# A vision block's head on one core: the state-space addition in two halves, and maxima over partitions by DMA rows and VectorE

## The reference

```python
# 1. tokens: a diagonal state-space kernel, for each token h and example c a row of 1024
K = 2.0 * einsum('chn,hnl->chl', Cc, exp(dtA[:, :, None] * ell)).real        # h = (64, 128, 1024)
# 2. attention over the 128 tokens of each example, 32 heads of 32, 8 key/value heads, rope
h = h + attention(layernorm(h), wq, wk, wv, wo)
# 3. a dense layer with LoRA experts and a router
y = x @ W_base.T + b_base
contribs = (x @ lora_A[active].T) @ lora_B[active].T * 2.0
alpha = softmax(log(prior[active] + EPS) + (x @ router_W.T + router_b)[active])
h = h + y + sum(alpha * contribs)                                            # x here is layernorm(h)
```

## Time and profile before

| | |
|---|---|
| median of 3 executions | 3023.05 us (3019.66 to 3023.64) |
| the profiled execution | 3020.96 us, span 3019.1 us |
| mean granted TensorE clock | 0.973 |
| busy: TensorE, VectorE, ScalarE, GpSimd | 2840.1, 2468.1, 1897.5, 1968.4 us |

### The profile page before, as it was taken

How to read it: one execution, slowest core, us unless ns; L and a number is a source line. 1 busy time by engine, 2 the same in 40 slices (tenths; PEclk the granted TensorE clock), 3 DMA queues, 4 the chain that set the end, 5 groups by cost and what they waited for, 6 DMA issues and landing times.

```text
span 3019.1 us, 61979 instructions
## 1 busy us (share of the span) xinstructions
PE 2840.1 (94%) x16986; PEld 1410.7 (47%) x16986; DVE 2468.1 (82%) x8692; ACT 1897.5 (63%) x5933; POOL 1968.4 (65%) x1723
## 2 busy tenths in 40 slices
PE   3777699999999999999999999999999999999986
PEld 3555444444444444444444444444444444444432
DVE  7897578888888888888888888888888888888872
ACT  5775566666666666666666666666666666666651
POOL 3431377677677676677776677777777777767762
PEclk8988699999999999999999999999999999999998
DMA  7965466766666667666667666666666766666651
GB/s 199 214 173 164 88 139 145 145 146 153 147 142 151 150 143 153 147 146 148 146 145 152 148 147 148 146 150 147 151 149 140 152 146 146 152 147 145 143 121 53
DMA packets 1252719, 442.59 MB, mean 147 GB/s; under 512 B 1200144, under 2 KB 1208592, under 8 KB 1252512
## 3 DMA queue, kind: packets, MB, share of 16 engines
q1 hardware_dynamic: 1252512, 440.69, 66.2%
HBM read 88.22 MB, written 67.11 MB: 51 GB/s over the span
## 4 chain that ended last, share of the span: by engine, by line
PE 43%; DVE 21%; issue 13%; POOL 12%; ACT 8%; SPq 1%; DMA 1%; DVEq 1%; ACTq 0%; POOLq 0%
PE bank_b L1570 19%; PE bank_a L1570 13%; DVE heads L1363 5%; ACT probs L1166 5%; DVE probs L1309 5%; POOL p_hl L1085 4%; POOL probs L1081 4%; PE bank_c L1570 3%; PE kps L498 2%; PE score L1537 2%; POOL rope_a L1091 2%; DVE share L1318 2%; PE pv L1559 1%; POOL xy_hl L1100 1%; POOL z L262 1%
## 5 line engine op out<-in xcount | busy, mean ns | idle before, releaser
L1166 ACT ACTIVATE probs<-probs,negmax 128x128 f32<-128x128 f32 x2048 | 789.8, 387 | 262.5 <-DVE negmax L1309 262.4
L1085 POOL TENSOR_TENSOR p_hl<-probs,p_hl 128x512 f16<-128x512 f32 x512 | 615.7, 1203 | 344.6 <-ACT p_hl L1175 342.3
L1081 POOL TENSOR_TENSOR probs<-probs,rsum 128x512 f32<-128x512 f32 x512 | 556.7, 1087 | 221.4 <-DVE rsum L1320 220.3
L1570 PE MATMUL bank_a<-qkv_hi,xt 128*128 128x512 f16 x2048 | 653.5, 381 | 2.0 <-DMA xt<-xy_hl 2.0
L1570 PE MATMUL bank_b<-b_hi,yt 128*128 128x512 f16 x2048 | 643.3, 381 | 0.0
L1309 DVE CUSTOM_DVE_ANT_0 probs<-score,table,scal 128x128 f32<-128x128 f32 x2048 | 599.3, 348 | 45.7 <-issue 44.9
L1175 ACT ACTIVATE p_hl<-probs 128x512 f16<-128x512 f32 x512 | 319.9, 625 | 421.1 <-POOL probs L1081 412.8
L1363 DVE TENSOR_TENSOR heads<-rope_a,heads 128x512 f16<-128x512 f32 x320 | 400.4, 1267 | 27.7 <-ACT heads L1196 27.7
L1570 PE MATMUL bank_b<-b_lo,yt 128*128 128x512 f16 x1024 | 390.0, 381 | 0.0
L1570 PE MATMUL bank_a<-qkv_lo,xt 128*128 128x512 f16 x1024 | 389.5, 380 | 0.0
L1570 PE MATMUL bank_b<-o_hi,at_hi 128*128 128x512 f16 x1024 | 388.1, 379 | 0.0
(11 more groups left out here) (204 smaller groups left out, 4597.0 us busy)
## 6 DMA issues: line engine op xcount, KB each, us to landing
tok_h<-kout SPq DMA_DIRECT2D x64, 512.0 KB, 5.9
hin<-tok_h SPq DMA_DIRECT2D x64, 512.0 KB, 3.3
r<-tok_h SPq DMA_DIRECT2D x64, 512.0 KB, 3.8
out_dram<-r SPq DMA_DIRECT2D x64, 512.0 KB, 2.9
probs_t<-p_hl SPq DMA_TRANSPOSE x512, 3.1
xc<-in_x_dram SPq DMA_DIRECT2D x32, 128.0 KB, 4.1
raw_a<-in_L_attn_wq_dram SPq DMA_DIRECT2D x1, 4096.0 KB, 13.4
raw_b<-in_L_attn_wo_dram SPq DMA_DIRECT2D x32, 128.0 KB, 3.6
```

Source lines behind the costliest of these rows:

```text
L1081: TT(x, x, rsum[:, u % 4].unsqueeze(2).to_broadcast([P, GR, T]), ALU.mult).then_inc(s_norm, 1)
L1085: TT(p_hl[:, u % 2, 1], probs[:, u % 4], p_hl[:, u % 2, 0], ALU.subtract).then_inc(s_plo, 1)
L1166: ins = A(probs[:, u % 4, g], probs[:, u % 4, g], ACT.Exp, bias=negmax[:, u % 4, g:g + 1], scale=-1.0, accum_out=sums[:, u % 4, g:g + 1])
L1570: ins = MM(bank, x(c), w[:, c, cols], start=(c == 0 and i == 0), stop=(c == KC - 1 and i == 2))
```

## The change

- **The addition in halves.** GpSimd adds `z2` into `z` in two instructions of four steps each, with a count after each; TensorE waits for the first before step 0 and for the second before step 4.
- **Maxima.** `partition_all_reduce` is gone everywhere. The column of 128 maxima `mx` is stored as a row to DRAM (`row_out`), loaded to all partitions (`row_in`, `wide`), and VectorE reduces the row to one value in `powers`. All ten DMAs are issued by SyncE, each `row_in` waits for its `row_out`.
- **wo's maximum.** Its eight reductions leave the bodies of chunks 12 to 14 and stand in `begin`, behind the first two low parts.
- **Order and banks.** TensorE turns two weight blocks, then does the last chunk's rows, then the lora_b product. The ring has the banks 0, 1, 4, 7 up to job 32 and 0, 1, 4 up to job 40. The scales 1 and 4 and the LoRA B parts (`lbs`) move behind the norm of example 0 (`after`). The router's scale and parts move two steps later in example 0. `lb` lies in the buffer of the bias, whose load (`bias_load`) now comes behind W_base and LoRA A.

```diff
-    sb("fill_ar", [P, KC * AR])
+    wide = sb("wide", [P, 2, P])
+    sb("fill_ar", [P, KC * AR - 2 * P])
...
         for ch in range(-1, NCH):
             body(ch, ch % 2)
+            if ch == NCH - 3:
+                prep.row_out(sp, 0, 1)
+            if ch == NCH - 2:
+                prep.row_in(sp, 0)
...
-                nc.gpsimd.tensor_tensor(z[:, r], z[:, r], z2[:, r], ALU.add).then_inc(s_z, 1)
+                for i in range(2):
+                    half = slice(CH // 2 * i, CH // 2 * (i + 1))
+                    nc.gpsimd.tensor_tensor(z[:, r, half], z[:, r, half], z2[:, r, half], ALU.add).then_inc(s_z, 1)
...
-            if isinstance(ch, int) and ch == NCH - 3:
-                maximum(0)
...
-            if isinstance(ch, int) and NCH - 4 <= ch < NCH - 1:
-                dve.wait_ge(w["wo_in"], 16 * HQ)
-                for i in range(3 * (ch - NCH + 4), min(3 * (ch - NCH + 4) + 3, NO)):
-                    part_maximum(slice(NQ + i, NQ + i + 1), raw_b[:, i])
...
         def rows(ch, r, h0, h1):
-            pe.wait_ge(s_z, ch + 1)
             pe.wait_ge(s_v, ch + 1)
             for h in range(h0, h1):
+                if h % 4 == 0:
+                    pe.wait_ge(s_z, ch * 2 + (h // 4 + 1))
...
+        def row_out(sp, i, count):
+            sp.wait_ge(s_mx, count)
+            sp.dma_start(rows_of[i:i + 1].rearrange("o p -> p o"), mx[:, i:i + 1]).then_inc(s_row[i], 16)
+
+        @staticmethod
+        def row_in(sp, i):
+            sp.wait_ge(s_row[i], 16)
+            sp.dma_start(wide[:, SLOT[i]], rows_of[i:i + 1].to_broadcast([P, P])).then_inc(s_wide[i], 16)
...
+            def powers(i):
+
+                m, p, s = mxa[:, i:i + 1], scal[:, P_QKV + i:P_QKV + i + 1], scal[:, i:i + 1]
+                dve.wait_ge(s_wide[i], 16)
+                scale_step(V.tensor_reduce(m, wide[:, SLOT[i]], AX_X, ALU.max))
...
             def begin():
-                dve.wait_ge(s_all, 1)
-                powers(0, 1)
+                powers(0)
...
+                low(0, 2)
+                dve.wait_ge(w["wo_in"], 16 * HQ)
+                for i in range(NO):
+                    part_maximum(NQ + i, raw_b[:, i])
+                whole_maximum(1, NQ, NQ + NO)
+                low(2, 4)
...
+            def after():
+                low(14, 20)
+                powers(1)
...
+            Prep.turn(pe, 0, 2)
+            rows(0, CH)
+            Prep.turn(pe, 2, 4)
             pe.wait_ge(s_sel, 1)
...
-                if attention and not some(b):
-                    prep.all_reduce(pool, 3, 3)
...
-                if qkv and not attention:
-                    prep.all_reduce(pool, 2, 2)
...
+                if qkv and not attention:
+                    prep.row_out(sp, 2, 4)
```

More of the change, by code:

```diff
@@ L23 @@
 LH = L0 // 2
-FILL = 200
+FILL = 1224
 HQ, HKV, HD = 32, 8, 32
@@ L113, in token_kernel @@
     qb = sb("qb", [P, 1])
-    lb = sb("lb", [P, KC, NE, R])
     sb("fill_qkv", [P, FILL])
@@ L531, in prepare_weights @@
     s_sel = sem("selection_ready")
-    s_all = w["s_all"]
-    s_lmx = sem("later_maxima_by_partition")
-    s_bpart = sem("w_base_part_maxima")
+    s_mx = w["s_mx"]
+    s_part = sem("matrix_part_maxima")
+    s_row = [sem(f"maxima_row_stored{i}") for i in range(5)]
+    s_wide = [sem(f"maxima_row_loaded{i}") for i in range(5)]
+    s_bias = sem("bias_loaded")
     s_sc = sem("scale_step")
@@ L561, in prepare_weights, with bank @@
     TENSOR = {"qkv": 0, "o": 1, "b": 2}
+    def bank(j):
+        if j < MID:
+            return (0, 1, 4, 7)[j % 4]
+        return (0, 1, 4)[(j - MID) % 3] if j < J_B else 2 + j % 2
     def place(j):
-        return ring[j % 4 if j < J_B else 2 + j % 2]
+        return ring[bank(j)]
+    before, last = {}, {}
+    for j in range(len(jobs)):
+        before[j] = last.get(bank(j), -1) + 1
+        last[bank(j)] = j
+        if j == MID - 1:
+            last_c = last[7]
+    SLOT = {0: 0, 1: 1, 4: 0, 2: 1, 3: 0}
     class Prep:
-        wlo, wt, lbs, ar_done = s_wlo, s_wt, s_lbs, s_arlo
+        wlo, wt, lbs, ar_done, bias, ps = s_wlo, s_wt, s_lbs, s_arlo, s_bias, s_ps
+        done_c, done_score = last_c + 1, (last[0] + 1, last[1] + 1)
         jb, jend, mid = J_B, J_END, MID
@@ L629, in act_open @@
                                  scale=scal[:, S_LB:S_LB + 1]).then_inc(s_lbt, 1)
-            copies(4, 8)
-            Prep.high(act, 2, 19)
+            Prep.high(act, 22, MID)
         @staticmethod
@@ L640, in act_early @@
                 Prep.high(act, MID + 4, J_B)
-            if b == 0 and k == 2:
+            if b == 0 and k == 4:
                 act.wait_ge(s_scal[4], 1)
@@ L720, in begin @@
                 ins.then_inc(s_lbs, 1)
-                low(2, 16)
             def base_maxima(i0, i1):
@@ L759, in early @@
                     low(J_B + 2 * k, J_B + 2 * k + 2)
-            return select, begin, low, early
+            return select, begin, after, early
         @staticmethod
@@ L790, in pe_open @@
             ins.then_inc(s_ps, 1)
+            Prep.turn(pe, 4, 6)
             pe.wait_ge(s_lb, 16 * KC)
+            pe.wait_ge(s_pr, 1)
             for c in range(KC):
@@ L794, in pe_open @@
             ins.then_inc(s_lbt, 1)
-            Prep.turn(pe, 0, 2)
+            Prep.turn(pe, 6, 10)
             pe.wait_ge(s_lbt, 2)
@@ L800, in pe_open @@
             ins.then_inc(s_ps, 1)
-            rows(0, CH)
-            Prep.turn(pe, 2, MID)
+            Prep.turn(pe, 10, MID)
         @staticmethod
@@ L808, in pe_close @@
             pe.wait_ge(s_la, 32)
+            pe.wait_ge(s_wlo, last[4] + 1)
             for c in range(KC):
@@ L1025, in turn @@
                     turn_heads(b, 3)
+                if attention and not some(b):
+                    prep.row_out(sp, 3, 5)
                 if rest:
@@ L1036, in turn @@
                     turn_probs(b, 0)
+                if attention and not some(b):
+                    prep.row_in(sp, 3)
+                if attention:
                     turn_probs(b, 1)
@@ L1049, in turn @@
                     sp.wait_ge(s_xlo, m + 1)
+                    if not qkv:
+                        sp.wait_ge(prep.ps, 2)
                     await_(sp, s_q, n * 2 + 2 if qkv else 0)
@@ L1052, in turn @@
                                            xy_hl[:, :, :].rearrange("p a k -> p (a k)")).then_inc(s_xt, 16)
+                if qkv and not attention:
+                    prep.row_in(sp, 2)
                 if qkv:
@@ L1132, in turn @@
                     pool.wait_ge(s_yhi, f + 1)
+                    if not some(f):
+                        pool.wait_ge(prep.bias, 16)
                     TT(r[:, par], r[:, par], keep["bias"][:, :], ALU.add).then_inc(s_bias, 1)
@@ L1281, in _ @@
             at(turn, -2)
-            prep.high(act, 19, prep.mid)
+            prep.act_after(act)
             turns(act, turn)
@@ L1286, in _ @@
         def _(dve):
-            select, begin, low, early_of = prep.dve_tools(dve)
+            select, begin, after, early_of = prep.dve_tools(dve)
             token_vector(dve, select)
@@ L1510, in _ @@
             at(turn, -2)
-            low(16, prep.mid)
+            after()
             V.memset(small[:, :], 2.0 ** -14).then_inc(s_small, 1)
@@ L1593, in q @@
                         await_(pe, s_rope, n * 3)
+                        if not some(n):
+                            pe.wait_ge(prep.wlo, prep.done_c)
                         if finish:
@@ L1730, in vit_tower_kernel @@
         with ExitStack() as banks:
-            ring = [banks.enter_context(nc.psum_tensor(f"wt{i}", [P, 4, P], F32)) for i in range(4)]
+            ring = [banks.enter_context(nc.psum_tensor(f"wt{i}", [P, 4, P], F32)) for i in range(8)]
+        with ExitStack() as banks:
+            banks.enter_context(nc.psum_tensor("before_ar", [P, 4, 512], F32))
             ps_ar = banks.enter_context(nc.psum_tensor("ps_ar", [P, KC, AR], F32))
```

111 lines of the change are left out of this document (59 added, 52 removed).

## The result

The changed kernel takes 2995.44 us in the median of four runs (2991.80 to 2995.78), beside 3022.57 for the kernel before, measured together with it: a ratio of 0.9914, with a 95% interval of 0.9902 to 0.9927. It is 0.9% faster, inside the range and 5 us above the 2990 that I gave. The profiled execution is the fastest of the four (2991.80, span 2990.0) and 2.4 above the sum of the prediction (2989.4). Its first scores start at 300.02 instead of 328.14; the span is 29.1 shorter, so nearly the whole gain lies ahead of them.

A forecast was written before the change was run, and what follows sets the result against it. Bounds: TensorE from 480 us; in the token loop a chain of GpSimd's addition, TensorE's products and VectorE, with VectorE next. Loop and start 12 plus 19.6 to first scores, 31.6 off 3020.96: 2989.4, predicted median 2990, range 2980 to 3004.

The forecast's parts named there:

- The loop: Token stage up to chunk 12: half additions of 2.25, VectorE's 22.87 a round as floor; 12 us gained with the start.
- SyncE's slack: Loop: 1.05 us in a short round; as floor, five rounds save less, 1.9 at best, giving 11.7 instead of 13.3.
- Rival (b): The loop gives almost nothing, copies waiting for landed stores: 3 instead of 12, total 2999; chance 0.20.
- The tail: From v of chunk 12 to example 0's norm: v of 15 at 32, last copy about 45; gain 11.9 at the norm.
- Row 0: First scale's maxima row: in by 31 to 34, covered by the last addition; uncovered, up to 2 us.
- row 4: Weights part, lora_b's maxima row: a maximum until 57.6; two scales end 1.3 behind the high parts; no transfer time given.
- Rival (d): Slower: SyncE's ordered queue exposes round trips, 5.8 each, some 13 behind stores; four wholly exposed 52, total 3042; chance 0.04.
- the covers above: Work said to hide small transfers: last addition, row 2 seven us early, xt six, TensorE's products; cited against the slower rival.
- row 2: W_base's maxima row, before the first scores: leaves at 100, in by 106, seven us before VectorE asks.
- To the first scores: First product to first scores: example 1's power no longer waits 15.6; scores at 113.1, gain 19.6, ends 14 and 25.
- rival (c): TensorE granted 2.4 GHz in the tail: 4.2 at the router's product, 1.13 in three long rounds; total 2982; chance 0.12.
- The sum: Whole kernel: 12+19.6=31.6 us off the profiled 3020.96 gives 2989.4; median 2.1 above, so 2990.

The follow-up runs named there:

- e3: Changed kernel with the first four loads of W_base issued behind maxima row 4's round trip; 2994.77 us, ratio to the kernel before 0.9911.
- e4: Changed kernel with lora_b's scale and two parts behind all qkv blocks, row 4's load behind the transposition of example 0's norm; 2991.74 us, ratio 0.9907.
- e8: e4 with, in addition, all loads of W_base issued behind the transposition of example 0's norm; 2988.18 us, ratio to the kernel before 0.9887.
- e1: Kernel before the change with GpSimd's addition in two halves and nothing else; 3007.50 us, ratio to the kernel before 0.9953.
- e6: Changed kernel with W_base's maximum over partitions made by GpSimd again, without maxima row 2; 3011.18 us, ratio to the kernel before 0.9963.

## Why the prediction was right, and where not

**The loop.** Halves of 2.25: 2.34. Rounds of 23 to 24: 23.3, with VectorE as the floor. Gain at the end of v of chunk 12, with the start, 12: 14.0 in the profiled execution (195.45 to 181.41), 9.4 and 10.3 in the two other traces of the same loop, 13.3 with the halves alone. The mechanism was right, and the size lies in the spread; what I booked as 1.9 less for SyncE's slack is in truth an occasional stumble, 2 to 3.5 us in a whole loop, which the profiled run was spared. That would fit with the median 3.6 above this run, but only this one of the four has a trace. Rival (b) said that the copies would wait for landed stores. They do, but this takes up a third of the loop's gain at most.

**The tail.** v of chunk 15 ends at 32.3 behind that of chunk 12 (I said 32), the last copy at 44.5 (45), the eight reductions at 46.2 (49.1), the norm of example 0 at 60.3 (60.3). This last is right by two errors. VectorE was ready at 57.2, since its small product in the first scale was held for 0.50 only and not until the whole addition ends, 3.5; then it waited 3.07 for hin, which I had there by 56. (Row 0, which the held product was to cover, was 1.15 late.) The gain is 11.9, as said, but its last step is the stores' landing, not VectorE.

**The failed step: row 4.** The prediction has "VectorE's two scales end 1.3 later", with no wait before them: it gives row 4 neither a time to leave nor a time to be in, so its trip stands at nothing. By the price that I had, "A load of 128 words lands in 2.5 us", "a round trip costs at least 2x2.5 plus issues, 5.8", and with its maximum at 57.6 it would have been in at 63.4, some 7 before it was asked for. But the row is a load to 128 partitions, and I priced with it a store from 128 partitions and a load of 64 KB. Three things add up in the trace. Alone the two cost 7.1 to 7.5 and 4.7 to 5.0, some 12 in all and not 5.8. In place the way out took 12.25, of which 4.4 are gone when W_base's loads stand behind it (7.88 in e3). And the way out stood 4.6 in SyncE's queue behind row 1's way in. So the scales, forecast 1.3 behind the high parts at 71.2, were ready at 77.6, and the gain forecast at the first product, 7.3, was 0.2 (84.8 behind the end of v of chunk 12, against 85.0); the two other traces, with waits of 4.67 and 4.13 for row 4 instead of 6.22, have the product at 82.0 and 81.0. e4 shows that it was this: with row 4 off the path the product starts at 77.1, where I had 77.7, though its last step is now the transposition. Rival (d) had the mechanism, and even the price when exposed (13 behind stores; 17.4 in place for row 4), but set against it "the covers above", and above there was none for row 4. Of the covers that it does name, that of row 2, "seven before VectorE asks", was 1.24 short, and that of row 0 1.15.

**To the first scores.** From the first product on 35.4 were forecast and 33.9 measured (before 47.7): the power's wait is gone as said, and the router's product took 6.7 instead of 8.5, its first part with pairs of matmuls of 0.38 to 0.41 us at a granted clock of 1.00 (2.4 GHz) and its second with 0.58 to 0.64 at 0.50 (1.2 GHz), where before nearly all took 0.58 to 0.64 at 0.50. Ahead of it TensorE had idled 5.49 us before the last turns, before the change 18.31. This is a piece of rival (c), 1.8 of its 4.2. First scores: 118.6, forecast 113.1; the two other traces have 116.8 and 114.7, e4 has 113.2 and e8 112.6.

**The sum.** First scores gained 28.1 where 31.6 were forecast: 2.0 more in the loop, the same at the norm, 7.1 less at the first product, 1.6 more behind it. From the first scores to the end the span is 1.0 shorter. So 29.2 in the profiled pair, and 23.6 to 27.1 in the medians. That the profiled execution comes within 2.4 of the sum is in part luck: a loop without a stumble made up for some of row 4.

## What to carry to other kernels

Price a transfer by its form and direction, from a transfer of the same form: a few hundred bytes gathered from 128 partitions do not cost what the same bytes scattered to them do. If no row shows it, the upper bound is the uncovered one; give each transfer a time to leave, with what stands ahead of it in its queue, and a time to be in, and ask its cover how long it is. When a wait is taken out of a loop, read the DMA share of the round first: at 0.89 there is little left for a round that becomes 9% shorter, and the loop ran as forecast in four of eleven traces. A large load that is issued ahead of a small transfer on the path can cost the path: here W_base's loads made row 4's way out 2.5 to 4.4 us longer, and the first transposition took 11.63 behind four of them.

## What the runs showed of the hardware

The way of one word per partition to DRAM takes 7.1 to 7.5 us with nothing beside it, a word to each partition from DRAM 1.96, and the same bytes from one partition to DRAM 1.09.

GpSimd holds a two-input operation of VectorE only until its current instruction ends: the small product that stood 3.01 against a whole addition stood 0.50 against the halves (215.71 to 216.21; the first half, 2.34 from 213.82, ends at 216.16), though the second half followed at once. So it is in all ten traces with the halves and this order: the product stands 0.42 to 1.73 and ends 0.03 to 0.05 behind the first half (2.34 from the addition's start). The Trainium skill (SBUF — State Buffer, SBUF: two separate sides) has the shared pair of ports as a lock that is held for the whole instruction; by that rule both traces come out, and the prediction had stretched it to a pair of instructions. The gap between the halves has a price on the other side: in e1, where a two-input operation of VectorE stood ready at the end of the first half of chunk 14's addition, the second half took 3.32 us instead of 2.34, and the two together 5.63 instead of 4.67.

GpSimd pays on the way back from its maximum: 7.26 before, 7.51 in e1 and 6.80 in e6 before the next plain operation, with nothing in the trace that releases it. It pays on the way in as well, and not the first time alone: 5.81 and 6.02 before, 5.73 and 5.99 in e1, between an addition and the maximum behind it.
